# Four buffers for split weight parts, raw parts in the raw weights' place, and all attention constants ahead of batch 0

## The chip, the cores and the metric

One Trainium2 chip, one core of it. The metric is the device time of one execution in microseconds. The core's engines are TensorE (PE, with its weight loads as PEld), VectorE (DVE), ScalarE (ACT), GpSimd (POOL) and SyncE (SP), which here issues all transfers.

## What is computed

A macaron block over x of shape (8, 512, 256):

```python
x = x + 0.5 * ffn(layernorm(x), ...)
x = x + attention(layernorm(x), ...)
x = x + 0.5 * ffn(layernorm(x), ...)

# ffn: weights rounded to an 8-bit float, 256 -> 768 -> 256
gate = silu((x @ q(gate_w)) * gate_scale)
up = (x @ q(up_w)) * up_scale
return ((gate * up) @ q(down_w)) * down_scale

# attention: 16 heads of 128; q, k, v = silu(conv4(x @ W)); per token and head
sk = einsum('bhij,bhj->bhi', St, k_)
Sn = a_ * St - b_ * (sk - v_) k_^T
o_ = einsum('bhij,bhj->bhi', Sn, q_)
# then a norm over the head, a gate sigmoid(x @ Wg), and @ Wo
```

## The kernel before

The stream of eight batches of 512 tokens stays in SBUF. There are two phases, each a block with one instruction list for each engine; the order of every list is written out by hand, and semaphores join them. The second phase (`attention_phase`) runs the attention in steps of 128 tokens by four heads, with the last feed-forward layer in its tail. The change doesn't touch it.

`first_phase` runs the first feed-forward layer and, one or two batches behind, the second norm and the decay rows. Its unit is `turn(b)`, one for each engine and batch:

- DVE first converts the three feed-forward weights (`wraw` to `wq16`, 1536 columns each, six instructions each, at L474 to L481), with `low(0, 0)` and `stats(0, 1)` between the first and the second. Then it takes statistics, multiplies gate and up (`hidden`, L388), and scales the down product (L399).
- PE does `gate`, `up` (L642) and `down` (L660) for six tiles of 128 hidden columns a batch, and transposes (L614). `down(b, m)` needs POOL's lower half of the hidden tile, and there are three hidden buffers.
- ACT normalises (L508), takes silu (L528), and rounds the hidden tile to 16 bits (`hidden_high`, L537).
- POOL computes the roots for the norms (`root`, L298 to L303), the lower half of each hidden tile (`low`, L311), and adds the result to the stream (`added`, L321).

Beside this the attention's weights are split into two 16-bit halves. There are 20 parts of 128 x 1024 columns, three a turn. SP loads part x into `raw[:, x % 4]` (L182); ACT writes the upper half (`part_high`, L555) and DVE the lower one (`part_low`, L438). Parts 0 to 4 go straight into the attention's tiles; the others go to `pairs[:, x % 2]`, from which SP stores them in HBM (`save_part`, L190). ACT's part x waits for the store of part x - 2. In ACT's list `part_high(b + 1, 0)` stands between `high(0, b + 1)` and `normed(0, b + 2)`, and silu of the next batch comes behind them.

POOL also makes the constants of the attention phase: `attention_constants` (12 instructions: identities, a first mask, zeros of 3072 16-bit columns in `y16`) behind turn 0, and `level_constants(li)` (six levels, 10 instructions each) behind each of turns 1 to 6. Each of these instructions waits for the one before (`chain`). A level builds its mask in `blocks` (32 bits) and copies it to a 16-bit tile.

Of the kernel before, what the change touches and what calls it, by code (L numbers as in the profile page):

```python
# [61 lines left out]
def first_phase(nc, x_in, stream, z16, kit, scratch, w):  # L62

    with ExitStack() as ctx:
        def sb(name, shape, dt=F32):
            return ctx.enter_context(nc.sbuf_tensor("f_" + name, shape, dt))

        def sem(name):
            return ctx.enter_context(nc.semaphore("f_" + name))
# [30 lines left out]
        wabh = sb("wabh", [P, KT, 2 * NH], F16); wabl = sb("wabl", [P, KT, 2 * NH], F16)  # L100
        bab = sb("bab", [2 * NH, 1])
        ab = sb("ab", [2 * NH, 2, NC, CX]); gx = sb("gx", [NH, 2, NC, CX])
        heads0 = sb("heads0", [NH, NC, CX]); blocks = sb("blocks", [P, P])
        raw = sb("raw", [P, RAW, PART]); pairs = sb("pairs", [P, 2, 2, PART], F16)

        def of_norms(name):

# [3 lines left out]
        s_x = [sem(f"dma_tokens{i}") for i in range(3)]  # L111
        s_out = [sem("dma_out0"), sem("dma_out1")]
        s_save = sem("dma_saved"); s_wd = sem("weights_ready"); s_prm = sem("dma_conv")
        s_part = [sem(f"dma_part{i}") for i in range(RAW)]; s_pair = [sem("dma_pair0"), sem("dma_pair1")]
        a_part = sem("act_part"); d_part = sem("dve_part")
        s_const = sem("constants"); s_q = sem("quantise_step"); s_made = sem("pool_made")
        p_z = of_norms("pe_z")
# [17 lines left out]

        def part_pair(x):

            return pair_tiles(kit, x) if x < KINDS else pairs[:, x % 2]

        def part_of(b, k):  # L140

# [9 lines left out]
        @block.sync  # L151
        def _(sp):
            def load_x(b):
                sp.dma_start(stream[:, b], x_tok[b]).then_inc(s_x[min(b, 2)], 16)

            def load_columns(dst, name):
                sp.dma_start(dst[:, :], w[name].rearrange("(m p) -> p m", p=P),
                             allow_slow_non_contiguous=True).then_inc(s_small, 16)

            def store_rows(b):  # L160

                if b < 0:
                    return
                g = b % 2
                sp.wait_ge(d_ab, b + 1)
                for h in range(HG):
                    sp.dma_start(a_to[h, b], ab[U * h:U * (h + 1), g]).then_inc(s_out[g], 16)
                sp.wait_ge(d_g, b + 1)
                for h in range(HG):
                    sp.dma_start(g_to[h, b], gx[U * h:U * (h + 1), g]).then_inc(s_out[g], 16)  # L170

            def load_part(x):

                group, kind = divmod(x, KINDS)
                dst = raw[:, x % RAW]
                if kind < KINDS - 1:
                    src = w[("Wk", "Wq", "Wv", "Wg")[kind]].rearrange("(k p) (g n) -> g p k n", p=P, g=HG)[group]
                    dst = dst.rearrange("p (k n) -> p k n", k=KT)
                else:
                    src = w["Wo"].rearrange("(g u p) n -> g p u n", p=P, u=U)[group]  # L180
                    dst = dst.rearrange("p (u n) -> p u n", u=U)
                sp.dma_start(dst, src).then_inc(s_part[x % RAW], 16)  # L182

            def save_part(x):

                if x is None:
                    return
                sp.wait_ge(d_part, x + 1)
                if x >= KINDS:
                    sp.dma_start(w_pairs[x], pairs[:, x % 2]).then_inc(s_pair[x % 2], 16)  # L190
                if x + RAW < PARTS:
                    load_part(x + RAW)

            load_x(0)
            for i, (name, rows) in enumerate((("gate_w", KT), ("up_w", KT), ("down_w", MT))):
                sp.dma_start(wraw[:, i * KT * FF:(i + 1) * KT * FF].rearrange("p (k n) -> p k n", k=rows),
                             w[name].rearrange("(k p) n -> p k n", p=P)).then_inc(s_w[i], 16)
                if i == 0:
                    load_x(1)
            sp.dma_start(wab[:, :, 0:NH], w["Wa"].rearrange("(k p) n -> p k n", p=P)).then_inc(s_small, 16)  # L200
            sp.dma_start(wab[:, :, NH:], w["Wb"].rearrange("(k p) n -> p k n", p=P)).then_inc(s_small, 16)
            sp.dma_start(bab[0:NH, :], w["ba"].rearrange("(p o) -> p o", o=1)).then_inc(s_small, 16)
            sp.dma_start(bab[NH:, :], w["bb"].rearrange("(p o) -> p o", o=1)).then_inc(s_small, 16)
            load_columns(gs, "gate_scale")
            load_columns(us, "up_scale")
            sp.dma_start(hds[:, :], w["down_scale"].rearrange("(o n) -> o n", o=1).broadcast_to([P, H]))\
                .then_inc(s_small, 16)
            for b in range(2, B):
                load_x(b)
            for i, k in enumerate("kqv"):  # L210
                sp.dma_start(prm[:, i, :, 0:TAPS], w[k + "cw"].rearrange("(h p) t -> p h t", p=P))\
                    .then_inc(s_prm, 16)
                sp.dma_start(prm[:, i, :, TAPS], w[k + "cb"].rearrange("(h p) -> p h", p=P),
                             allow_slow_non_contiguous=True).then_inc(s_prm, 16)
            for x in range(RAW):
                load_part(x)
            sp.wait_ge(s_wd, 4)
            sp.dma_start(w_saved, wq16[:, :]).then_inc(s_save, 16)
            sp.dma_start(lnwn[:, :], w["ln_w"].rearrange("(p o) -> p o", o=1)).then_inc(s_prm, 16)
            sp.dma_start(lnb[:, :], w["ln_b"].rearrange("(p o) -> p o", o=1)).then_inc(s_prm, 16)  # L220
            for t in range(1, B + 2):
                save_part(part_of(t, 0))
                store_rows(t - 2)
                save_part(part_of(t, 1))
                save_part(part_of(t, 2))
            sp.wait_ge(s_save, 16)
            sp.wait_ge(s_prm, 16 * 8)
            for g in range(2):
                sp.wait_ge(s_pair[g], 16 * len([x for x in range(KINDS, PARTS) if x % 2 == g]))
                sp.wait_ge(s_out[g], rows_stored(B // 2))  # L230

        @block.gpsimd
        def _(pool):
# [14 lines left out]
            def chain(ins):  # L248

                made[0] += 1  # L250
                ins.then_inc(s_made, 1)
                pool.wait_ge(s_made, made[0])

            def fill(out, value, test, base, pattern, mult):
                chain(nc.gpsimd.affine_select(out=out, in_=out, compare_op=test, fill=value, base=base,
                                              pattern=pattern, channel_multiplier=mult))
# [17 lines left out]

            def level_constants(li):

                if not 0 <= li < NL:
                    return
                mb, y16 = LEVELS[li], kit["y16"]
                nb = P // (2 * mb)  # L280

                blk = blocks[:, :].rearrange("p (b two m) -> p b two m", two=2, m=mb)[:, :, 0, :]
                chain(nc.gpsimd.memset(blocks[:, :], 0.0))
                chain(nc.gpsimd.memset(blk, -1.0))
                fill(blk, 0.0, ALU.is_ge, -mb, [[-2 * mb, nb], [0, mb]], 1)
                fill(blk, 0.0, ALU.is_ge, 2 * mb - 1, [[2 * mb, nb], [0, mb]], -1)
                fill(blocks[:, :], -1.0, ALU.not_equal, 0, [[-1, P]], 1)
                chain(nc.gpsimd.tensor_copy(kit["masks"][:, li].rearrange("p (b m) -> p b m", m=mb), blk))
                for u in range(U):
                    chain(nc.gpsimd.tensor_copy(halves(y16[:, li, u], mb, 1), halves(kit["ident"][:, :], mb, 1)))  # L290

            def root(n, e):

# [39 lines left out]
                added(b)  # L333

            root(0, 0)
            root(0, 1)
            for b in range(0, B + 2):
                turn(b)
                if b == 0:
                    attention_constants()  # L340
                level_constants(b - 1)

        @block.vector
        def _(dve):
# [156 lines left out]
        def _(act):  # L501
# [46 lines left out]
            def part_high(b, k):  # L548
                x = part_of(b, k)
                if x is None:  # L550
                    return
                act.wait_ge(s_part[x % RAW], 16 * (x // RAW + 1))
                if x >= KINDS + 2:
                    act.wait_ge(s_pair[x % 2], 16 * len(range(KINDS + (x - KINDS) % 2, x, 2)))
                nc.scalar.activation(part_pair(x)[:, 0], raw[:, x % RAW], ACT.Copy, scale=WS).then_inc(a_part, 1)  # L555

            def turn(b):
# [1508 lines left out]
def pair_tiles(kit, x):  # L2066

    group, kind = divmod(x, KINDS)
    if kind < 3:
        return kit["kqv16"][:, :, kind].rearrange("p w k u d -> p w (k u d)")  # L2070
    if kind == 3:
        return kit["gate16"][:, :].rearrange("p w k u d -> p w (k u d)")
    return kit["wo16"][:, group % WO_SLOTS].rearrange("p w u n -> p w (u n)")
# [48 lines left out]
```

## Time and profile before

| | |
|---|---|
| median of 3 runs | 2467.68 us (2467.63 to 2468.91) |
| the profiled execution | 2468.06 us |
| its span | 2466.3 us |
| mean granted TensorE clock | 0.987 |
| busy of the span: PE, DVE, ACT, POOL | 96%, 82%, 74%, 74% |
| first phase | to about 238 us |

The span runs from the first to the last instruction of the core. A granted clock of 1.00 is 2.4 GHz and 0.50 is 1.2 GHz. Busy time of an engine says nothing by itself of what bounds a stage; idle time with what ended it, in the order of time, does.

### The profile page before, as it was taken

What the parts mean: (1) busy time and instruction counts of PE and PEld (TensorE: products, weight loads), DVE (VectorE), ACT (ScalarE), POOL (GpSimd) and SP (SyncE); (2) the same over time, 40 slices, a digit from 0 to 9 for tenths busy, and PEclk for the clock granted to TensorE, in tenths of its full rate; (3) what the DMA queues carried; (4) which work ended last, traced back from release to release, by engine and by line L of the source; (5) the groups of instructions that cost most, each with busy time, mean ns of one, the idle gap of its engine ahead of it and who ended that gap; (6) DMA issues with size and microseconds to landing.
All of it is one profiled execution on the core that took longest, in us unless ns stands there. A gap on an engine that the chain in (4) does not pass through costs nothing.

```text
span 2466.3 us, 64137 instructions
## 1 busy us (share of the span) xinstructions
PE 2357.2 (96%) x24496; PEld 1827.6 (74%) x24496; DVE 2017.2 (82%) x4246; ACT 1817.0 (74%) x3566; POOL 1818.9 (74%) x1973
## 2 busy tenths in 40 slices
PE   5897899999999999999999999999999999997898
PEld 2554578788888878888888888888788787886655
DVE  7775888888888888888888888888888888885453
ACT  3674677777777777777777777777777777775564
POOL 3774577777777777777877777777877777776565
PEclk9998999999999999999999999999999999998999
DMA  6241011111121111111211111111211121111001
GB/s 165 88 146 45 27 32 28 27 32 32 32 58 49 32 32 32 32 31 29 49 57 32 32 32 30 29 28 40 66 32 32 36 46 28 29 32 22 12 27 44
DMA packets 72833, 103.59 MB, mean 42 GB/s; under 512 B 21456, under 2 KB 33744, under 8 KB 72400
## 3 DMA queue, kind: packets, MB, share of 16 engines
q1 hardware_dynamic: 72528, 99.48, 15.9%
q8 instruction: 197, 3.23, 0.5%
q14 instruction: 108, 0.88, 0.1%
HBM read 85.69 MB, written 13.77 MB: 40 GB/s over the span
## 4 chain that ended last, share of the span: by engine, by line
PE 81%; DVE 6%; issue 1%; POOL 1%; ACT 1%; DVEq 0%; POOLq 0%; ACTq 0%
PE a_bank L1887 25%; PE a_bank L1867 7%; PE a_bank L1676 5%; PE a_bank L1690 5%; PE a_bank L1829 5%; PE a_bank L1828 4%; PE a_bank L1811 3%; PE a_bank L1722 3%; PE a_bank L1736 3%; PE a_bank L1734 3%; PE a_bank L1957 3%; DVE a_prod L1140 3%; PE a_bank L1759 2%; PE a_bank L1846 2%; PE a_bank L1749 2%; PE a_bank L1699 2%
## 5 line engine op out<-in xcount | busy, mean ns | idle before, releaser
L1887 PE MATMUL a_bank<-k_z,k_kqv 128*128 128x512 f16 x2304 | 597.9, 380 | 10.7 <-DVE a_kb L1233 4.2
L1462 ACT ACTIVATE a_inv<-a_bank 128x512 f16<-128x512 f32 x640 | 383.4, 599 | 216.9 <-PE a_bank L1736 201.5
L1164 DVE TENSOR_TENSOR k_y<-a_bank,k_masks 128x256 f16<-128x256 f32 x768 | 318.7, 415 | 134.9 <-PE a_bank L1722 131.1
L1887 PEld LDWEIGHTS a_bank<-k_z,k_kqv 128*128 128x128 f16 x2304 | 197.9, 98 | 139.8 <-DVE a_kb L1233 6.2
L912 POOL TENSOR_TENSOR k_diag<-k_ident,k_bcol 128x512 f32<-128x512 f32 x128 | 133.0, 1039 | 224.1 <-DVE a_prod L1140 209.1
L1233 DVE SCALAR_TENSOR_TENSOR a_kb<-a_bank,k_prm,a_kb 128x511 f32<-128x511 f32 (+2 forms) x384 | 282.7, 737 | 14.6 <-ACT a_kb L1406 14.3
L1233 DVE SCALAR_TENSOR_TENSOR a_vb<-a_bank,k_prm,a_vb 128x511 f32<-128x511 f32 (+2 forms) x384 | 283.7, 739 | 0.1
L1233 DVE SCALAR_TENSOR_TENSOR a_qb<-a_bank,k_prm,a_qb 128x511 f32<-128x511 f32 (+2 forms) x384 | 282.8, 737 | 0.5 <-ACT a_qb L1406 0.3
L1736 PE MATMUL a_bank<-a_inv,k_y 128*128 128x64 f16 x3072 | 271.8, 193 | 3.8 <-DVE k_y L1164 3.8
L1734 PE MATMUL a_bank<-k_y,a_inv 128*128 128x64 f16 x2560 | 236.5, 193 | 5.6 <-DVE k_y L1164 3.1
L1722 PEld LDWEIGHTS a_bank<-a_inv,a_am 128*128 128x128 f16 x3072 | 169.1, 98 | 92.6 <-ACT a_inv L1462 2.0
L1736 PEld LDWEIGHTS a_bank<-a_inv,k_y 128*128 128x128 f16 x3072 | 207.4, 98 | 37.6 <-DVE k_y L1164 4.6
L1734 PEld LDWEIGHTS a_bank<-k_y,a_inv 128*128 128x128 f16 x2560 | 197.4, 98 | 44.6 <-DVE k_y L1164 18.5
L924 POOL TENSOR_TENSOR a_am<-a_at,k_ident 128x512 f16<-128x512 f32 x128 | 163.6, 1278 | 80.6 <-DVE a_at L1149 80.6
L1000 POOL TENSOR_SCALAR a_gb<-a_gb 128x512 f32<-128x512 f32 x128 | 219.6, 1716 | 1.2 <-ACT a_gb L1426 1.2
L1722 PE MATMUL a_bank<-a_inv,a_am 128*128 128x64 f16 x3072 | 215.9, 193 | 1.4 <-ACT a_inv L1462 1.2
L1887 PE MATMUL a_bank<-k_z,k_gate 128*128 128x512 f16 x768 | 200.8, 379 | 0.2 <-DVE a_vb L1233 0.2
L1487 ACT ACTIVATE a_on<-a_bank,a_shift,a_rstd 128x128 f32<-128x128 f32 x512 | 192.2, 463 | 0.7 <-POOL a_shift L992 0.7
L1867 PE MATMUL a_bank<-k_wo,a_oh 128*128 128x256 f16 x1024 | 189.3, 273 | 2.1 <-POOL a_ol L1016 2.1
L1829 PE MATMUL a_bank<-a_wv,a_mix 128*128 128x128 f32 x1024 | 185.8, 279 | 0.7 <-DVE a_wv L1183 0.7
L1140 DVE TENSOR_TENSOR_SCAN a_prod<-a_decay,k_diag 128x516 f32<-128x516 f32 x128 | 181.9, 1421 | 2.1 <-ACT a_kdec L1437 2.1
L1009 POOL TENSOR_TENSOR a_oa<-a_oa,a_gb 128x512 f32<-128x512 f32 x128 | 163.1, 1274 | 21.0 <-ACT a_oa L1496 17.3
(178 smaller groups left out, 6638.7 us busy)
## 6 DMA issues: line engine op xcount, KB each, us to landing
a_decay<-decay_rows SPq DMA_DIRECT2D x128, 258.0 KB, 3.7
a_cum<-cumulative_rows SPq DMA_DIRECT2D x96, 258.0 KB, 3.6
weight_pairs<-f_pairs SPq DMA_DIRECT2D x15, 512.0 KB, 2.9
k_kqv<-weight_pairs SPq DMA_DIRECT2D x9, 512.0 KB, 4.8
stream<-in_L_attn_x SPq DMA_DIRECT2D x8, 512.0 KB, 7.1
out<-stream SPq DMA_DIRECT2D x8, 512.0 KB, 2.9
f_raw<-in_L_attn_Wk SPq DMA_DIRECT2D x4, 512.0 KB, 4.7
f_raw<-in_L_attn_Wq SPq DMA_DIRECT2D x4, 512.0 KB, 5.1
```

Of the source, the lines that this page charges most:

```text
L1000: nc.gpsimd.tensor_scalar(gb[:, n % 2, j], gb[:, n % 2, j], 1.0, None, ALU.add).then_inc(m["pool_one"], 1)
L1140: nc.vector.tensor_tensor_scan(prod[:, :], decay[:, :], diag[:, :, :].rearrange("p u x -> p (u x)"), 0.0, ALU.mult, ALU.add).then_inc(m["d ...
L1164: nc.vector.tensor_tensor(even(y16[:, j], mb), bank[LEV[par]][:, 0:U * C // 2].rearrange("p (u b m) -> p u b m", u=U, m=mb), masks[:, j].r ...
L1233: nc.vector.scalar_tensor_tensor(out=dst[:, d:S], in0=bank[PJ[j % 2]][:, 0:S - d], scalar=prm[:, i, U * (n // B) + j, TAPS - 1 - d:TAPS - ...
L1462: nc.scalar.activation(both, bank[LEV[par]][:, :].rearrange("p (two b m) -> p two b m", two=2, m=mb), ACT.Copy).then_inc(m[f"act_lev{par}" ...
L1487: ins = nc.scalar.activation(on[:, u], bank[OUT][:, u * D:(u + 1) * D], ACT.Identity, bias=shift[:, u:u + 1], scale=rstd[:, u:u + 1])
L1722: mm = pe.matmul(at_half(LEV[par], 0, u), am16[:, par, u], halves(t16[par][:, u], mb, 0), start=True, stop=True)
L1734: pe.matmul(at_half(LEV[par], 0, u), tt16[par][:, u], halves(y16[:, j, u], mb, 0), start=True, stop=True)
L1736: mm = pe.matmul(at_half(LEV[par], half, u), y16[:, j, u], halves(tt16[par][:, u], mb, 1), start=True, stop=True)
L1829: mm = pe.matmul(units(OUT)[:, u], mix[:, t % 2, u], wv[:, u], start=not c, stop=True)
L1867: mm = pe.matmul(bank[SUM][:, 0:H], o[:, u], wo16[:, group % WO_SLOTS, wh, u], start=(u == 0 and wh == 0 and o is oh), stop=(u == U - 1 an ...
L1887: mm = pe.matmul(bank[PJ[j % 2]][:, :], wt, z16[:, zh, k, cols], start=(x == 0), stop=(x == 5))
```

## The change

Three edits in the first phase. `pairs` has four buffers where it had two, with a semaphore each. `raw`, which was a tensor of its own, becomes the first 4096 columns of `wraw`, so that the loads of the first four raw parts now stand behind SP's wait for the converted feed-forward weights. POOL makes all constants ahead of its turns: the shared ones and level 0 between the roots of batch 0 and batch 1, the other five levels behind the root of batch 1. A level now builds its mask in the 16-bit tile itself (8 instructions where there were 10) and copies the 16-bit identity.

```diff
-        heads0 = sb("heads0", [NH, NC, CX]); blocks = sb("blocks", [P, P])
-        raw = sb("raw", [P, RAW, PART]); pairs = sb("pairs", [P, 2, 2, PART], F16)
+        heads0 = sb("heads0", [NH, NC, CX])
+        raw = wraw[:, 0:RAW * PART].rearrange("p (r n) -> p r n", r=RAW); pairs = sb("pairs", [P, RAW, 2, PART], F16)
...
-                    sp.dma_start(w_pairs[x], pairs[:, x % 2]).then_inc(s_pair[x % 2], 16)
+                    sp.dma_start(w_pairs[x], pairs[:, x % RAW]).then_inc(s_pair[x % RAW], 16)
...
+            sp.wait_ge(s_wd, 4)
             for x in range(RAW):
                 load_part(x)
-            sp.wait_ge(s_wd, 4)
             sp.dma_start(w_saved, wq16[:, :]).then_inc(s_save, 16)
...
             def level_constants(li):
...
-                chain(nc.gpsimd.memset(blocks[:, :], 0.0))
-                chain(nc.gpsimd.memset(blk, -1.0))
-                fill(blk, 0.0, ALU.is_ge, -mb, [[-2 * mb, nb], [0, mb]], 1)
-                fill(blk, 0.0, ALU.is_ge, 2 * mb - 1, [[2 * mb, nb], [0, mb]], -1)
-                fill(blocks[:, :], -1.0, ALU.not_equal, 0, [[-1, P]], 1)
-                chain(nc.gpsimd.tensor_copy(kit["masks"][:, li].rearrange("p (b m) -> p b m", m=mb), blk))
+                mask = kit["masks"][:, li].rearrange("p (b m) -> p b m", m=mb)
+                chain(nc.gpsimd.memset(mask, -1.0))
+                fill(mask, 0.0, ALU.is_ge, -mb, [[-2 * mb, nb], [0, mb]], 1)
+                fill(mask, 0.0, ALU.is_ge, 2 * mb - 1, [[2 * mb, nb], [0, mb]], -1)
+                fill(mask, -1.0, ALU.not_equal, 0, [[-2 * mb, nb], [-1, mb]], 1)
                 for u in range(U):
-                    chain(nc.gpsimd.tensor_copy(halves(y16[:, li, u], mb, 1), halves(kit["ident"][:, :], mb, 1)))
+                    chain(nc.gpsimd.tensor_copy(halves(kit["y16"][:, li, u], mb, 1),
+                                                halves(kit["ident16"][:, :], mb, 1)))
...
             root(0, 0)
+            attention_constants()
+            level_constants(0)
             root(0, 1)
+            for li in range(1, NL):
+                level_constants(li)
             for b in range(0, B + 2):
                 turn(b)
-                if b == 0:
-                    attention_constants()
-                level_constants(b - 1)
...
-                if x >= KINDS + 2:
-                    act.wait_ge(s_pair[x % 2], 16 * len(range(KINDS + (x - KINDS) % 2, x, 2)))
+                if x >= KINDS + RAW:
+                    act.wait_ge(s_pair[x % RAW], 16 * ((x - KINDS) // RAW))
```

## Rows read from the trace of the kernel before

**Rows 1.** Windows between starts of the adds: length, busy of each engine (instructions), clock, DMA.

```profile
54.40:77.02 22.62, 19.36 (x114) 11.56 (x113) 14.43 (x31) 16.25 (x29) 18.10 (x28) 0.92 0.13 44
77.02:100.63 23.61, 20.96 (x128) 12.10 (x126) 17.81 (x35) 17.15 (x29) 19.58 (x26) 1.00 0.23 73
100.63:123.96 23.33, 21.93 (x128) 12.73 (x126) 17.93 (x35) 14.04 (x23) 17.89 (x26) 0.93 0.37 121
123.96:148.02 24.06, 21.96 (x128) 12.73 (x127) 17.83 (x35) 16.91 (x28) 17.37 (x26) 0.93 0.43 132
148.02:171.96 23.94, 21.95 (x128) 12.75 (x127) 17.83 (x35) 16.96 (x28) 17.27 (x26) 0.93 0.43 139
171.96:194.11 22.15, 20.27 (x128) 12.26 (x127) 16.98 (x29) 16.85 (x28) 15.30 (x23) 1.00 0.43 139
194.11:215.96 21.85, 19.77 (x120) 11.26 (x119) 14.88 (x25) 12.84 (x21) 15.68 (x23) 1.00 0.20 75
```

**Rows 2.** Timeline of PE: start, us, instruction, idle before it and its releaser.

```profile
44.73 0.27 PE L660 MATMUL f_bank<-f_wq,f_hh 128*128 128x256 f16 x1
...
64.15 0.40 PE L660 MATMUL f_bank<-f_wq,f_hh 128*128 128x256 f16 x1 [2.69 <-POOL f_hl L311]
...
127.93 0.62 PE L642 MATMUL f_bank<-f_zh,f_wq 128*128 128x512 f16 x2 [2.10 <-ACT f_sg L528]
128.38 1.03 PE L642 MATMUL f_bank<-f_zl,f_wq 128*128 128x512 f16 x2
...
175.71 0.61 PE L642 MATMUL f_bank<-f_zh,f_wq 128*128 128x512 f16 x2 [1.88 <-ACT f_sg L528]
```

**Rows 3.** Timeline of ACT, two conversions of weight parts.

```profile
51.98 1.06 ACT L555 ACTIVATE k_kqv<-f_raw 128x1024 f16<-128x1024 f32 x1
...
124.28 1.06 ACT L555 ACTIVATE f_pairs<-f_raw 128x1024 f16<-128x1024 f32 x1 [2.62 <-DMA weight_pairs<-f_pairs]
```

**Rows 4.** The page's transfers: count, KB each, median us to landing.

```profile
weight_pairs<-f_pairs SPq DMA_DIRECT2D x15, 512.0 KB, 2.9
...
f_raw<-in_L_attn_Wk SPq DMA_DIRECT2D x4, 512.0 KB, 4.7
```

**Rows 5.** Timeline of DVE and POOL in the first 40 us.

```profile
16.28 1.29 DVE L379 TENSOR_TENSOR f_zl<-f_bank,f_zh 128x512 f16<-128x512 f32 x2 [0.90 <-ACT f_zh L520]
...
20.18 0.99 DVE L475 TENSOR_SCALAR f_wexp<-f_wexp 128x1536 f32<-128x1536 f32 x1
20.43 1.60 POOL L301 TENSOR_TENSOR f_rstd<-f_var,f_nhalf 128x4 f32<-128x4 f32 x1
21.20 1.76 DVE L476 TENSOR_TENSOR f_wraw<-f_wraw,f_wexp 128x1536 f32<-128x1536 f32 x1
22.11 0.91 POOL L303 TENSOR_TENSOR f_shift<-f_nmean,f_rstd 128x4 f32<-128x4 f32 x1
...
34.14 1.76 DVE L481 TENSOR_TENSOR f_wq<-f_wraw,f_wexp 128x1536 f16<-128x1536 f32 x1
...
38.53 1.15 POOL L311 TENSOR_TENSOR f_hl<-f_hid,f_hh 128x512 f16<-128x512 f32 x1 [15.51 <-ACT f_hh L537]
```

**Rows 6.** Timelines of POOL and DVE around the constants.

```profile
56.84 0.21 POOL L261 MEMSET k_ident<- 128x128 f32 x1
...
58.50 2.66 POOL L265 MEMSET k_y<- 128x3072 f16 x1
...
60.20 1.21 DVE L438 SCALAR_TENSOR_TENSOR k_kqv<-f_raw,k_kqv 128x1024 f16<-128x1024 f32 x1
...
62.94 1.15 POOL L311 TENSOR_TENSOR f_hl<-f_hid,f_hh 128x512 f16<-128x512 f32 x1
...
100.63 3.48 POOL L321 TENSOR_TENSOR stream<-stream,f_scaled 128x512 f32<-128x512 f32 x2 [1.91 <-DVE f_scaled L399]
101.07 1.92 DVE L438 SCALAR_TENSOR_TENSOR f_pairs<-f_raw,f_pairs 128x1024 f16<-128x1024 f32 x1
...
106.12 1.13 POOL L290 CAST k_y<-k_ident 128x64 f16<-128x64 f32 x4
```

More of the change, by code:

```diff
@@ L113, in first_phase @@
         s_save = sem("dma_saved"); s_wd = sem("weights_ready"); s_prm = sem("dma_conv")
-        s_part = [sem(f"dma_part{i}") for i in range(RAW)]; s_pair = [sem("dma_pair0"), sem("dma_pair1")]
+        s_part = [sem(f"dma_part{i}") for i in range(RAW)]; s_pair = [sem(f"dma_pair{i}") for i in range(RAW)]
         a_part = sem("act_part"); d_part = sem("dve_part")
@@ L136, in part_pair @@
         def part_pair(x):
-            return pair_tiles(kit, x) if x < KINDS else pairs[:, x % 2]
+            return pair_tiles(kit, x) if x < KINDS else pairs[:, x % RAW]
         def part_of(b, k):
@@ L227, in _ @@
             sp.wait_ge(s_prm, 16 * 8)
+            for x in range(RAW):
+                sp.wait_ge(s_pair[x], 16 * len([y for y in range(KINDS, PARTS) if y % RAW == x]))
             for g in range(2):
-                sp.wait_ge(s_pair[g], 16 * len([x for x in range(KINDS, PARTS) if x % 2 == g]))
                 sp.wait_ge(s_out[g], rows_stored(B // 2))
@@ L275, in level_constants @@
             def level_constants(li):
-                if not 0 <= li < NL:
-                    return
-                mb, y16 = LEVELS[li], kit["y16"]
+                mb = LEVELS[li]
                 nb = P // (2 * mb)
-                blk = blocks[:, :].rearrange("p (b two m) -> p b two m", two=2, m=mb)[:, :, 0, :]
-                chain(nc.gpsimd.memset(blocks[:, :], 0.0))
-                chain(nc.gpsimd.memset(blk, -1.0))
-                fill(blk, 0.0, ALU.is_ge, -mb, [[-2 * mb, nb], [0, mb]], 1)
-                fill(blk, 0.0, ALU.is_ge, 2 * mb - 1, [[2 * mb, nb], [0, mb]], -1)
-                fill(blocks[:, :], -1.0, ALU.not_equal, 0, [[-1, P]], 1)
-                chain(nc.gpsimd.tensor_copy(kit["masks"][:, li].rearrange("p (b m) -> p b m", m=mb), blk))
+                mask = kit["masks"][:, li].rearrange("p (b m) -> p b m", m=mb)
[3 more added lines that the diff above has]
+                fill(mask, -1.0, ALU.not_equal, 0, [[-2 * mb, nb], [-1, mb]], 1)
                 for u in range(U):
-                    chain(nc.gpsimd.tensor_copy(halves(y16[:, li, u], mb, 1), halves(kit["ident"][:, :], mb, 1)))
+                    chain(nc.gpsimd.tensor_copy(halves(kit["y16"][:, li, u], mb, 1),
+                                                halves(kit["ident16"][:, :], mb, 1)))
             def root(n, e):
```

## The prediction

> **What bounds the kernel now.** I read the page first, then busy time cut at the moments where POOL starts to add a batch's feed-forward result to the stream, then the timelines of PE, ACT, POOL and DVE with what each waited for, and last the transfers. The change touches only the first phase, the first 238 us or so. From 238 us on, where the long attention phase runs with its own order, no instruction differs, so I take that part as fixed and look for the difference in when the first phase ends.
>
> [Rows 1] give the turns of that phase, one batch each: 22.62, 23.61, 23.33, 24.06, 23.94, 22.15 and 21.85 us. I call them turns 1 to 7; turn 0 ends at 54.40. In the sixth PE stands idle once, 1.88 us at its end [rows 2], and its granted clock is 1.00 throughout; 22.15 - 1.88 = 20.3 us is what I take as the length of a turn whose PE is never late and whose clock never drops. PE is the bound to which the turns can shrink: DVE is busy 17 to 18 us and ACT 14 to 17 us of each [rows 1].
>
> What keeps turns 2 to 6 above 20.3 us? At the ends of turns 3, 4 and 5 PE waits 2.10, 1.99 and 1.88 us (first and last of the three in [rows 2]) for ACT's silu tile. ACT is late there because converting a weight part stood 2.62 us in front of it, waiting for a store of split weights [rows 3]: the two buffers take turns, so a part waits for the store of the part two before it, and such a store takes 2.9 us from issue to landing [rows 4]. After the wait of 2.10 us the granted clock falls from 2.4 to 1.2 GHz: a pair of 512-column products takes 1.03 us where it took 0.62 us [rows 2], and turns 3 to 5 show a mean clock of 0.93 [rows 1]. A mean of 0.93 over 24 us is 1.7 us of clock lost.
>
> In turn 1 PE waits 2.69 us, until 64.15, for POOL's first lower half [rows 2]. POOL was making the attention constants from 56.84 to 62.94 [rows 6]; the clock falls after that too (0.92 for the turn).
>
> **The change, part by part.**
>
> *Four split buffers.* ACT's wait for the store of x-2 becomes one for x-4, stored more than a turn earlier, so it goes. Each of turns 2 to 6 falls towards 20.3 us. Small waits stay whose cause is neither edit, so I take 21.0 us. The five sum to 117.1 us now and to 105.0 then: 12.1 us gained. Turn 7 has no normalisation of a next batch and converts two parts; I take 0.6 us there. Together -12.7 us. Bounds: at 20.3 us each it is -16.2 us; if each turn gives back only its PE waits of about 2 us in turns 3 to 5, with the clock loss unchanged, -6 us.
>
> *Raw parts in the feed-forward raw weights' place.* The first four loads are issued behind the last conversion (its last long instruction ends at 35.90 [rows 5]; the small weights follow within about 1 us) instead of at about 31 us. Four issues later, w_saved and two small loads follow on SP's queue; nobody reads those before the sixth turn. A raw load lands 4.7 us after issue [rows 4]; even with four of them sharing the engines, all are there by about 46 us, and ACT first reads one at 51.98 [rows 3]. Cost 0, hidden behind turn 0; without that cover it would be some 10 us. Copying the 16-bit identity in place of the 32-bit one I also put at 0: the same 64 columns.
>
> *Constants ahead of batch 0's rows.* This removes 6.1 us of POOL (56.84 to 62.94) from the start of turn 1 and about 3.1 us from each later turn: the adds end at 104.11 (100.63 + 3.48) and level 1's last copy at 107.25 [rows 6]. Its new place is from 10.9 us, behind the first root. Without block memset and mask copy a level costs about 2.4 us, level 0, whose runs are two elements long, about 2.8 (estimates from the 3.1). Unhindered: 10.9 + 6.0 + 2.8 + 1.6 (root of batch 1) + 5 x 2.4 = 33.3 us, before POOL is first wanted at 38.53 [rows 5]: cost 0. That is one bound.
>
> I don't take it, because DVE converts the feed-forward weights until 35.9 us almost without a gap, and there POOL is held. The power issued at 20.43 under DVE's 20.18 to 21.17 ends at 22.03, 1.60 us for some 1.0 elsewhere; the multiply issued at 22.11 ends at 23.02, just after DVE's 21.20 to 22.96 [rows 5]. So one POOL instruction that reads goes in at each DVE boundary. A memset does not need this: 58.50 to 61.16 lies over DVE's 60.20 to 61.41 and both keep their lengths [rows 6].
>
> The sum: boundaries at about 12.6 and 13.6 us let in the first select and the copy. From 15.38 DVE waits, then reads PSUM (16.28 [rows 5]) and takes statistics, until about 19.2, one conversion instruction ahead of 20.18. In this gap the long memset and the other small ones and two selects pass: the shared constants are done at about 19. The next 12 boundaries take level 0's three selects and four copies, the root of batch 1 and two instructions of level 1. DVE is held in turn by each (its 1.21 us instruction took 1.92 beside POOL's adds [rows 6]); for 64 columns I take 0.1 us each, 1.2 us in all, so DVE ends the conversions at 37.1. The root of batch 1 ends at about 34.3, then ACT needs about 2.1 us to normalise and 0.7 us for the first silu: 37.1 too, so it delays nothing more. From 37.1 POOL runs freely: 1.9 us of level 1 and 4 x 2.4 give 48.6. First lower half: 38.53 becomes 48.6.
>
> That rule has a page: in the Trainium skill, "SBUF — State Buffer", section "Who interferes with whom", the port pair that VectorE and GpSimd share is a lock, and whoever starts first keeps it for the whole instruction. The power in [rows 5] disagrees, since DVE's 21.20 instruction kept its 1.76 us beside it; with full-length holds of 0.25 to 0.45 us the conversions would end some 2 us later and the forecast would be about 2 us higher.
>
> What is late next: everything from PE's first down product, at 44.73 [rows 2], on. PE has done all that lies before it and idles from about 45 us; the half is there at 49.75 (1.15 us [rows 5]). From that product to the adds was 9.7 us (44.73 to 54.40); the idle clock costs 1.7 us as in the turns above: the adds of turn 0 start at 61.1, 6.7 us late. Turn 1: PE was ready for the first half 7.1 us after the adds (64.15 - 2.69 - 54.40), so it is ready at 68.2, and the half is there, since POOL is free. From 64.15 to 77.02 was 12.9 us at a dropped clock, 11.2 without that: 79.4 against 77.02, so +2.4 us. The constants' places in turn 1 give back 4.3 us of the 6.7.
>
> **Sum:** +2.4 - 12.7 = -10.3 us. Against the profiled execution's own 2468.06 (span 2466.3) that is 2457.8; the median of the runs is 0.4 us lower, and I forecast **2458 us**.
>
> **Rivals.** Within 0.2%, 4.9 us, is what a measurement of this kernel can't tell from no change.
>
> *POOL is not held at the start.* For: unhindered it is done at 33.3 us. Against: the two held instructions of [rows 5]. Then turn 0 ends at 54.4, PE is ready at 61.5, turn 1 ends at 72.7 (-4.3), and -4.3 - 12.7 = -17: 2451 us. It also stands for a milder hold.
>
> *Another wait takes the place of the stores.* DVE holds 17 to 18 us of a 21 us turn and shares its inputs with POOL; the parts' lower halves run beside POOL's adds at 1.92 us. If turns 2 to 7 give 6 us only, the time is 2468.06 + 2.4 - 6 = 2464.5, about the edge of no change; with a start 2 us worse, 2466.5.
>
> *The constants cost more than they give (slower).* One mechanism: after 37.1 us some 30 selects and copies stand in front of the first lower half with no cover, and on 16-bit strided tiles their price is not in the trace (only 32-bit selects and 32-to-16 copies are). The gain of 10.3 us is gone when each costs 0.3 us more, twice today's; at 0.5 us more the time is about 2473. Against: copies that write 16 bits already cost what 32-bit selects do.
>
> *Nothing changes:* the stores' wait is removed but start and turns cancel. It is the middle of the second rival, and counted there.
>
> **How the numbers follow.** Forecast 0.48 (own range 2454 to 2463), no hold 0.16, another wait 0.28 (half of it over 2462.8), slower 0.08. Faster by over 0.2% (under 2462.8): 0.47 + 0.16 + some of the second rival, 0.69 together; within it 0.24; slower 0.07. The range from 2450 to 2467 leaves out the slow rival and the ends.
>
> **What would show it.** Right: no ACT wait on stores after the first four splits; turns 2 to 6 of 20.5 to 21.3 us with a clock near 1.00; selects and copies one to each conversion until 37 us; the first lower half near 48.6 us; the first phase ending 10 us earlier. Wrong: a first lower half before 40 us or after 54 us, conversions ending after 39 us, turns still above 22 us, or a different attention phase.

## The result and the profile after

The changed kernel takes 2457.88 us (median, 2455.13 to 2459.36) against 2467.65 us of the kernel before in the same measurement: a ratio of 0.9958, 95% interval 0.9945 to 0.9971. The forecast was 2458, so the total is right. Part of that is luck: the first phase gained 13.3 us where 10.3 were forecast, and 3.0 of them are not in the total. And the reason that was given for most of the gain was only one of two.

Busy time of the changed kernel, cut at the starts of POOL's adds (turns 1 to 7), then the rest of the first phase, then the second phase in three pieces (columns as in [rows 1]):

```profile
59.92:79.33 19.41, 17.82 (x114) 11.07 (x113) 14.35 (x31) 16.25 (x29) 14.15 (x17) 1.00 0.17 52
79.33:99.93 20.60, 20.18 (x128) 12.23 (x126) 17.54 (x35) 16.51 (x28) 14.44 (x17) 1.00 0.27 82
99.93:120.54 20.61, 20.27 (x128) 12.30 (x127) 17.54 (x35) 16.73 (x30) 14.45 (x17) 1.00 0.43 139
...
161.75:182.36 20.61, 20.27 (x128) 12.33 (x127) 16.41 (x29) 15.51 (x26) 13.53 (x13) 1.00 0.48 150
182.36:202.63 20.27, 19.57 (x120) 11.34 (x119) 15.18 (x25) 11.90 (x20) 12.04 (x13) 1.00 0.21 82
...
224.59:2141.18 1916.59, 1902.10 (x21098) 1522.86 (x21099) 1676.31 (x3561) 1493.88 (x2988) 1477.61 (x1544) 1.00 0.15 36
2141.18:2272.99 131.81, 116.68 (x1229) 95.55 (x1228) 95.31 (x218) 90.15 (x184) 90.65 (x101) 0.91 0.13 26
2272.99:2456.00 183.01, 162.76 (x1166) 107.39 (x1164) 82.46 (x176) 98.44 (x173) 106.97 (x116) 0.97 0.08 28
```

Against [rows 1]: turns 2 to 6 take 20.60 or 20.61 us each, for 22.2 to 24.1; PE is busy 20.27 of 20.61 us in turns 3 and 6, at a clock of 1.00; POOL's busy time in turns 2 to 5 was 17.3 to 19.6 us and is about 14.4. The same three pieces of the second phase in the kernel before, cut at the same instructions (the scan of the decays that is 121st and the last of the 128):

```profile
237.93:2154.28 1916.35, 1901.02 (x21098) 1522.79 (x21099) 1676.37 (x3562) 1495.41 (x2988) 1477.25 (x1544) 1.00 0.15 36
2154.28:2284.84 130.56, 114.39 (x1232) 94.00 (x1231) 95.32 (x218) 90.25 (x185) 90.67 (x101) 0.93 0.12 26
2284.84:2466.30 181.46, 160.80 (x1163) 106.15 (x1161) 82.35 (x176) 98.14 (x173) 106.98 (x116) 0.98 0.09 28
```

The second phase starts 13.34 us earlier (224.59 for 237.93), keeps all but 0.24 us of that over 1916 us, and gives back 1.25 and 1.55 us in its last two pieces, where the granted clock is 0.91 and 0.97 for 0.93 and 0.98. PE stands idle several times there, up to 5.07 us in one wait.

The front of the changed kernel, POOL's timeline:

```profile
18.77 2.66 POOL L256 TENSOR_SCALAR_AFFINE_SELECT k_masks<-k_masks 128x64 f16<-128x64 f16 x3
21.50 6.11 POOL L286 COPY k_y<-k_ident 128x64 f16<-128x64 f16 x4
27.70 0.87 POOL L295 TENSOR_TENSOR f_var<-f_mv,f_epsd 128x4 f32<-128x4 f32 x1
...
31.54 4.63 POOL L256 TENSOR_SCALAR_AFFINE_SELECT k_masks<-k_masks 128x64 f16<-128x64 f16 x3
36.23 1.21 POOL L286 COPY k_y<-k_ident 128x64 f16<-128x64 f16 x4
...
47.34 3.38 POOL L308 TENSOR_TENSOR f_hl<-f_hid,f_hh 128x512 f16<-128x512 f32 x3
```

and DVE's and PE's:

```profile
18.96 1.07 DVE L472 TENSOR_SCALAR f_wexp<-f_wraw 128x1536 int32<-128x1536 int32 x1
...
25.76 1.76 DVE L479 TENSOR_TENSOR f_wq<-f_wraw,f_wexp 128x1536 f16<-128x1536 f32 x1
...
34.19 1.76 DVE L479 TENSOR_TENSOR f_wq<-f_wraw,f_wexp 128x1536 f16<-128x1536 f32 x1
```

```profile
48.55 0.28 PE L658 MATMUL f_bank<-f_wq,f_hh 128*128 128x256 f16 x1 [4.10 <-POOL f_hl L308]
49.05 0.42 PE L658 MATMUL f_bank<-f_wq,f_hh 128*128 128x256 f16 x1
...
103.00 0.60 PE L640 MATMUL f_bank<-f_zh,f_wq 128*128 128x512 f16 x2 [0.34 <-DVE f_hid L386]
```

Four copies take 6.11 us where DVE converts and 1.21 us behind the last of them: POOL is held, as forecast, one reading instruction to a conversion. The first lower half comes at 47.34 us. DVE is hardly held in return: its two-input conversions keep 1.76 us, and the last ends at 35.95, 0.05 us later than before. (This stretch began 0.25 us earlier, so the conversions lost about 0.3 us.)

PE waits 4.10 us for that half and restarts at full clock, 0.28 us a product. Then the clock falls: until 52.4 us a product takes 0.42 us, and the mean granted clock from 48.55 to 52.41 is 0.56. From 48.55 to the adds at 59.92 it is 0.85, against 1.00 for the same work before. This work takes 11.37 us where it took 9.67. In turns 3 to 6 the only wait of PE is one of 0.34 us.

### The profile page after: what moved, and what is told of

Read it like the earlier page. It is cut to its first block, busy times and chain, and to the rows that moved or that the text cites. A ratio compares the mean times of both kernels' runs of the same rounds, so it can differ in the third digit from the quotient of the medians.

```text
span 2456.0 us, 64125 instructions
## 1 busy us (share of the span) xinstructions
PE 2354.8 (96%) x24496; PEld 1828.3 (74%) x24496; DVE 2015.9 (82%) x4246; ACT 1814.9 (74%) x3566; POOL 1824.1 (74%) x1961
## 4 chain that ended last, share of the span: by engine, by line
PE 81%; DVE 6%; issue 1%; POOL 1%; ACT 1%; DVEq 0%; POOLq 0%; ACTq 0%
PE a_bank L1885 25%; PE a_bank L1865 7%; PE a_bank L1674 5%; PE a_bank L1688 5%; PE a_bank L1827 5%; PE a_bank L1826 4%; PE a_bank L1809 3%; PE a_bank L1734 3%; PE a_bank L1720 3%; PE a_bank L1732 3%; PE a_bank L1955 3%; DVE a_prod L1138 3%; PE a_bank L1757 2%; PE a_bank L1844 2%; PE a_bank L1747 2%; PE a_bank L1697 2%
## 5 line engine op out<-in xcount | busy, mean ns | idle before, releaser
L1007 POOL TENSOR_TENSOR a_oa<-a_oa,a_gb 128x512 f32<-128x512 f32 x128 | 163.2, 1275 | 21.3 <-ACT a_oa L1494 17.3
```

## Experiments

All figures of this table but the last column are from the timelines of one profiled execution each; the time is a median of timed runs, and one run alone for the kernel with writes only. "Turns 2 to 6" is their sum. "First half" is the start of POOL's first lower half.

| kernel | first half | adds of turn 0 | turn 1 | turns 2 to 6 | first phase ends | time, us |
|---|---|---|---|---|---|---|
| before | 38.5 | 54.4 | 22.6 | 117.1 | 237.9 | 2467.44 to 2469.05 |
| changed | 47.3 | 59.9 | 19.4 | 103.0 | 224.6 | 2457.88; again: 2455.71 |
| raw parts' place alone | 38.2 | 54.3 | 22.6 | 115.4 | 236.2 | 2469.42 |
| buffers and place | 38.2 | 53.6 | 22.7 | 115.2 | 235.2 | 2466.94 |
| constants alone | 47.4 | 59.7 | 19.4 | 110.6 | 232.2 | 2464.22 |
| changed, levels 2 to 5 at the end | 38.7 | 53.7 | 19.4 | 103.0 | 218.5 | 2450.58 |
| changed, levels 1 to 5 twice | 60.0 | 73.2 | 19.4 | 103.0 | 238.2 | 2469.55 |
| changed, writes only | 38.4 | 53.9 | 19.4 | 103.0 | 218.6 | 2450.16 |
| levels 2 to 5 ahead of adds | 38.6 | 54.4 | 20.0 | 107.4 | 224.1 | 2456.51 |
| levels 2 to 5 behind adds | 38.6 | 53.7 | 19.4 | 110.9 | 226.2 | 2459.77 |

**Buffers without the constants.** The edits to `pairs`, `s_pair` and `raw`, on the kernel before; POOL's part as it was.

```diff
             root(0, 0)
-            attention_constants()
-            level_constants(0)
             root(0, 1)
-            for li in range(1, NL):
-                level_constants(li)
             for b in range(0, B + 2):
                 turn(b)
+                if b == 0:
+                    attention_constants()
+                level_constants(b - 1)
```

(against the changed kernel; `level_constants` is that of before)

> Four split buffers and the raw parts' new place, with the constants left where they were (behind turns 0 to 6). Theory 1 (the stores' wait is what lengthens turns 2 to 6): no ACT wait for a store, turn 1 stays 22.6 us with PE's wait of 2.7 us for the first lower half, turns 2 to 6 at about 20.9 us, first phase some 11 us shorter than before: about 2456.5 us. Rival (POOL's level constants at each turn's start would take the wait's place): turns 2 to 6 at about 22 us, about 2462 us.

Ratio to before 0.9993 (0.9984 to 1.0003): no difference that this measures, and neither theory. No ACT wait for a store is left, and yet turns 2 to 5 take 23.1 to 23.6 us. Windows of turns 3 and 4:

```profile
99.91:123.23 23.32, 20.78 (x128) 12.12 (x126) 17.81 (x35) 16.88 (x28) 19.28 (x26) 1.00 0.43 134
123.23:146.55 23.32, 20.79 (x128) 12.13 (x126) 17.82 (x35) 16.88 (x28) 19.29 (x27) 1.00 0.45 143
```

and rows of the turn from 146.55, all engines:

```profile
143.57 0.28 PE L661 MATMUL f_bank<-f_wq,f_hh 128*128 128x256 f16 x1 [0.93 <-POOL f_hl L312]
145.78 1.29 DVE L400 TENSOR_TENSOR f_scaled<-f_bank,f_hds 128x512 f32<-128x512 f32 x2 [1.56 <-PE f_bank L661]
146.55 3.48 POOL L322 TENSOR_TENSOR stream<-stream,f_scaled 128x512 f32<-128x512 f32 x2 [1.91 <-DVE f_scaled L400]
...
151.85 2.02 POOL L291 CAST k_y<-k_ident 128x64 f16<-128x64 f32 x4
153.95 1.15 POOL L312 TENSOR_TENSOR f_hl<-f_hid,f_hh 128x512 f16<-128x512 f32 x1
155.24 0.75 DVE L389 SCALAR_TENSOR_TENSOR f_hid<-f_bank,f_us,f_sg 128x512 f32<-128x512 f32 x1 [1.47 <-POOL f_hl L312]
156.82 2.07 ACT L509 ACTIVATE f_ztok<-stream,f_shift,f_rstd 128x256 f32<-128x256 f32 x4 [2.33 <-POOL f_shift L304]
...
163.63 1.84 POOL L304 TENSOR_TENSOR f_shift<-f_nmean,f_rstd 128x4 f32<-128x4 f32 x1
164.20 1.20 DVE L439 SCALAR_TENSOR_TENSOR f_pairs<-f_wraw,f_pairs 128x1024 f16<-128x1024 f32 x1
```

The waits that name POOL are now everywhere: PE 0.93 us, DVE 1.47 us, ACT 2.33 us. POOL is busy 19.3 us of the turn. Its longest wait, 1.91 us, is for the scaled product, which follows from its last lower half, and 1.06 us are for ACT's upper half of a hidden tile. So the chain runs through POOL around the turn: last half, down product, scaling, adds, constants, first half, root, next halves. What stands in it lengthens each turn.

Part of that chain is POOL being held by DVE. The multiply that ends a root takes 1.84 us here and ends 0.07 us after DVE's lower half of a weight part; the four copies took 2.02 us beside another such part. In the turns of the changed kernel this multiply takes 0.20 to 0.24 us, and four copies with nothing beside them take 1.13 us. No run takes this hold away alone, so its share of the 23.3 us is not shown.

**Constants without the buffers.** POOL's edit alone, on the kernel before.

```diff
-        raw = wraw[:, 0:RAW * PART].rearrange("p (r n) -> p r n", r=RAW); pairs = sb("pairs", [P, RAW, 2, PART], F16)
+        raw = sb("raw", [P, RAW, PART]); pairs = sb("pairs", [P, 2, 2, PART], F16)
```

(against the changed kernel, with the waits and SP's order of before)

> The constants ahead of batch 0 alone, with two split buffers and separate raw tiles. Theory 1: turn 0 ends 5.5 us later (59.9 for 54.4), turn 1 takes about 19.4 us for 22.6, turns 3 to 5 stay near 23.9 us because of the stores' wait: net +1 us, about 2468.5 us. Rival (the constants lengthened the turns, not the stores): turns 2 to 6 at 21 to 22 us and about 2461 us.

0.9984 (0.9975 to 0.9994), 4.8 us faster than before by the medians. Turns 0 and 1 are as theory 1 said (59.7, 19.4), the later ones are not. (The profiled execution, 2467.27 us, is the longest of its ten.) Turns 2 and 3 fall to 20.61 and 21.33 us: ACT's first wait for a store, 1.75 us, comes in turn 3. Turns 4 to 6 take 22.45, 22.40 and 23.84 us (the last at a clock of 0.93), with this wait in ACT and after it in PE:

```profile
143.62 1.06 ACT L552 ACTIVATE f_pairs<-f_raw 128x1024 f16<-128x1024 f32 x1 [2.65 <-DMA weight_pairs<-f_pairs]
...
147.28 0.60 PE L639 MATMUL f_bank<-f_zh,f_wq 128*128 128x512 f16 x2 [1.98 <-ACT f_sg L525]
```

Together, these two kernels settle where the gain came from. By the sum of turns 2 to 6, and against the 115.4 us of the kernel with the place alone, the buffers give 0.2 us, the constants 4.8, and both 12.4. (Against the one profile of the kernel before, 117.1 us, it is 1.9, 6.5 and 14.1.) Either of two causes is enough to keep a turn above 22 us.

**The raw parts' place alone.**

```diff
-        raw = sb("raw", [P, RAW, PART]); pairs = sb("pairs", [P, 2, 2, PART], F16)
+        raw = wraw[:, 0:RAW * PART].rearrange("p (r n) -> p r n", r=RAW); pairs = sb("pairs", [P, 2, 2, PART], F16)
...
+            sp.wait_ge(s_wd, 4)
             for x in range(RAW):
                 load_part(x)
-            sp.wait_ge(s_wd, 4)
```

> Raw parts in the feed-forward raw weights' place and nothing else. Theory 1: the first conversion of a part still finds its data, no time: 2467.7 us. Rival (later loads are late, or collide with the store of the converted weights): ACT waits for a raw part in turn 0 or 1, and 2470 us or more.

1.0002 (0.9992 to 1.0011): no time. No ACT wait for a raw part shows in turns 0 to 7. This kernel also shows how far one profiled execution of the kernel before can mislead: its turns 4 and 5 take 23.27 and 23.23 us with the clock at 1.00, where [rows 1] have 24.06 and 23.94 at 0.93. The longest ACT waits for a store are alike, 2.50 and 2.51 us for 2.51 and 2.40. So with the clock full these turns are 0.8 and 0.7 us shorter, not the 1.7 that the prediction reads from the clock, and what is left, 23.2 to 23.3 us, is about what the buffers alone leave too.

**The changed kernel again,** without an edit.

> The changed kernel again, for its last 220 us. Theory 1 (the granted clock falls at other moments in the last feed-forward stretch, and this is where 3 of the 13.3 us gained by 225 us went): the first phase ends within 0.3 us of the same time, the steps up to 2230 us keep their distance to it, and the runs differ by up to 4 us, the longer ones with the lower mean clock. Rival (the change costs 3 us in the second phase each time): the last stretch is as long in each run, and the total within 1 us of 2457.9.

2455.71 us (2454.78 to 2456.52), 0.9946 (0.9931 to 0.9961) of a kernel before that took 2469.05 there: 13.3 us, all that the first phase gained. The phase ends at 224.52, 0.07 us from the first time. Its second phase took 2230.2 us for 2231.4, and 1.05 us of the difference lie behind the last scan (181.96 us for 183.01). The runs of this measurement differ by 1.7 us, those of the first one by 4.2, and there the longest has a mean clock of 0.987 and the shortest 0.990. Over all profiled kernels, whose second phases hold the same instructions, that phase took 2228.4 to 2233.3 us. The kernel before that stands in [rows 1] is the shortest of them; the kernel with the place alone took 2230.0, like this one. So the 3 us are not a cost that the change has each time.

**Levels 2 to 5 at the end.**

```diff
-            for li in range(1, NL):
-                level_constants(li)
+            level_constants(1)
             for b in range(0, B + 2):
                 turn(b)
+            for li in range(2, NL):
+                level_constants(li)
```

> The changed kernel with levels 2 to 5 made behind the last turn, where POOL was idle for 15 us, instead of ahead of batch 0. Theory 1 (POOL's constants stand in front of the first lower half): the first lower half at 38.2 us for 47.3, turn 0 ends at 54.4 for 59.8, the turns stay at 20.6 us, the levels (9.7 us) fit in POOL's idle time, and the first phase ends 5.4 us earlier. Rival (the end has no room, or turn 1 takes the time back because its own waits grow): 0 to 2 us gained.

2450.58 us (2450.03 to 2453.14), 0.9928 of before (0.9914 to 0.9943): the fastest complete kernel of the study, 17 us under before. The first phase ends 6.1 us earlier. POOL's timeline:

```profile
36.26 1.21 POOL L286 COPY k_y<-k_ident 128x64 f16<-128x64 f16 x4
38.68 1.16 POOL L308 TENSOR_TENSOR f_hl<-f_hid,f_hh 128x512 f16<-128x512 f32 x1 [1.21 <-ACT f_hh L536]
...
203.40 0.15 POOL L281 MEMSET k_masks<- 128x64 f16 x1
...
212.09 1.14 POOL L286 COPY k_y<-k_ident 128x64 f16<-128x64 f16 x4
218.46 1.04 POOL L911 TENSOR_TENSOR k_diag<-k_ident,k_bcol 128x512 f32<-128x512 f32 x1 [5.23 <-POOLq L64]
```

Level 1 is done 1.21 us before the first half could start; the other four take 9.8 us at the end, and 5.23 us of idle time are left.

**Levels 1 to 5 twice.**

```diff
-            for li in range(1, NL):
+            for li in list(range(1, NL)) * 2:
```

> The changed kernel with levels 1 to 5 made twice ahead of batch 0, to double a suspected cost. Theory 1: the first lower half comes 12.1 us later, at 59.4 us, and the first phase ends 12 us later, one to one. Rival (PE has slack in turns 0 and 1 that takes part of it): 8 us or less.

The first half comes 12.7 us later and the phase ends 13.6 us later, 2469.55 us for 2457.88: one to one and a little more, and as slow as the kernel before (1.0006, 0.9997 to 1.0015). PE's first down product waits long and starts at the low clock already (0.40 us for 0.28):

```profile
61.23 0.40 PE L658 MATMUL f_bank<-f_wq,f_hh 128*128 128x256 f16 x1 [16.82 <-POOL f_hl L308]
```

**Writes only.** The selects and copies of the six levels are memsets on the same tiles; the masks and identities of the attention are left out.

```diff
                 chain(nc.gpsimd.memset(mask, -1.0))
-                fill(mask, 0.0, ALU.is_ge, -mb, [[-2 * mb, nb], [0, mb]], 1)
-                fill(mask, 0.0, ALU.is_ge, 2 * mb - 1, [[2 * mb, nb], [0, mb]], -1)
-                fill(mask, -1.0, ALU.not_equal, 0, [[-2 * mb, nb], [-1, mb]], 1)
+                for _ in range(3):
+                    chain(nc.gpsimd.memset(mask, -1.0))
                 for u in range(U):
-                    chain(nc.gpsimd.tensor_copy(halves(kit["y16"][:, li, u], mb, 1),
-                                                halves(kit["ident16"][:, :], mb, 1)))
+                    chain(nc.gpsimd.memset(halves(kit["y16"][:, li, u], mb, 1), 0.0))
```

> The changed kernel with all selects and copies of the six levels replaced by memsets on the same tiles (so the masks and identities of the attention are left out; its output is not the reference's). Theory 1 (POOL is held by DVE's conversions only where it reads SBUF, or where DVE runs a one-input conversion at double rate): level 0's four copies, 6.11 us before, take under 2 us, the root of batch 1 starts near 22 us for 27.7, and the first lower half is at 38.2 us. Rival (each POOL instruction is held, reading or not): one memset a conversion, the root near 27 us as before.

```profile
18.73 2.21 POOL L283 MEMSET k_masks<- 128x64 f16 x3
20.99 0.78 POOL L285 MEMSET k_y<- 128x64 f16 x4
21.86 0.84 POOL L293 TENSOR_TENSOR f_var<-f_mv,f_epsd 128x4 f32<-128x4 f32 x1
...
31.27 0.78 POOL L285 MEMSET k_y<- 128x64 f16 x4
...
38.37 1.16 POOL L306 TENSOR_TENSOR f_hl<-f_hid,f_hh 128x512 f16<-128x512 f32 x1 [0.46 <-ACT f_hh L533]
```

Theory 1 holds, both halves of it. Under DVE's conversions with two inputs in SBUF four memsets take 0.78 us where four copies took 6.11. Three memsets of 0.15 us take 2.21 us at 18.73, where DVE runs two one-input conversions of 1536 columns in 0.93 and 0.96 us: those hold writes too. The last conversion ends at 35.61 here; POOL's reading instructions cost DVE the 0.34 us up to 35.95.

The Trainium skill's "SBUF — State Buffer", section "Who interferes with whom", has it so: GpSimd's writes are free beside a VectorE instruction of two SBUF inputs and blocked beside one in a two-port mode. The traces agree, if the one-input conversions, 0.96 us for columns that take 1.76 with two inputs, are in such a mode.

**Levels 2 to 5 in front of the adds,** and then **behind them** (both with level 1 ahead of batch 0).

```diff
                 low(b, 5)
+                if 1 <= b <= NL - 2:
+                    level_constants(b + 1)
                 added(b)
```

```diff
             for b in range(0, B + 2):
                 turn(b)
+                if 1 <= b <= NL - 2:
+                    level_constants(b + 1)
```

> Shared constants and levels 0 and 1 ahead of batch 0, levels 2 to 5 in turns 1 to 4 in front of POOL's adds, where POOL waits 2.2 us for DVE. Theory 1 (what the constants cost in a turn is their place between the adds and the first lower half): turns 1 to 4 lengthen by 0.2 to 0.5 us each at most, and the first phase ends 4 to 5 us earlier than in the changed kernel. Rival (POOL's total work in a turn counts): turns 1 to 4 at 22 us or more.

> As the kernel with levels 2 to 5 in front of the adds of turns 1 to 4, but behind these adds, at the start of turns 2 to 5, where the kernel before had them. Theory 1 (POOL's chain through a turn sets its length as soon as 2.4 us more stand in it, four split buffers or not): turns 2 to 5 at 22.3 to 23.0 us, the others at 20.6, the first phase ending at about 226 us. Rival (place doesn't matter, the sum of POOL's work does): 21.8 us as in front of the adds, ending at 223.

In front of the adds, turns 1 to 4 carry a level: turn 1 takes 20.0 us, the others 21.7 to 21.8. Turn 5, with none, still takes 21.4. Behind the adds, turns 2 to 5 carry one and take 22.5 to 22.7 us. That is 1.2 and 2.0 us more than without. Two windows of each, in front and then behind:

```profile
74.45:96.19 21.74, 20.50 (x127) 12.17 (x126) 17.18 (x35) 16.83 (x29) 18.94 (x25) 1.00 0.24 76
96.19:118.00 21.81, 20.56 (x127) 12.25 (x126) 17.24 (x35) 16.71 (x29) 19.00 (x24) 1.00 0.47 146
```

```profile
73.09:95.77 22.68, 20.78 (x128) 12.18 (x126) 17.80 (x35) 17.15 (x29) 18.79 (x24) 1.00 0.25 76
95.77:118.34 22.57, 20.79 (x128) 12.18 (x126) 18.80 (x35) 16.88 (x28) 18.66 (x24) 1.00 0.47 138
```

For the behind case theory 1 is right (22.3 to 23.0 forecast, phase end 226.2 for 226). For the one in front both theories missed (0.2 to 0.5 us more a turn, and 22 us or more; the phase ends at 224.1, 0.5 us before the changed kernel's and not 4 to 5): POOL's idle time of 2.24 us before the adds doesn't take in a level of 2.4 us for nothing. The place matters, by 0.8 us. POOL is busy 18.7 to 19.0 us in both, 4.2 to 4.6 more than in the changed kernel, though a level is 2.4: in turns 2 to 5 of both the multiply of a turn's second root takes 1.84 us for 0.20, also in turn 5 of the first kernel, where no level is left. So a POOL that is late also meets DVE's weight parts; that this is what lengthens turn 5 is likely, not shown.

Behind the adds, a level of 8 instructions (22.6 us a turn) stands against one of 10 in the buffers without the constants (23.3). Making a level shorter gives 0.7 us of the 2.7, taking it out of the turn the other 2.0.

## Why the prediction came out as it did

**Right, and shown.** The POOL side of the start: one reading instruction to a conversion, memsets passing beside the two-input conversions, the first half at 47.3 us (48.6), turn 0's adds at 59.9 (61.1), turn 1's at 79.3 (79.4). Doubling the levels moved the end one to one, and taking them out from in front of the first half gave 6.1 us back and 2450.6 us, near the 2451 that the prediction gives for a turn 0 that ends at 54.4. The clock after PE's first wait also fell as forecast: the work up to the adds took 1.70 us more, for 1.7. The new place of the raw parts costs nothing. The turns do shrink to what PE needs: 20.6 us, between the 20.3 and 21.0 that were weighed.

**Mis-sized, same mechanism.** DVE's conversions: about 0.3 us longer in all, not 1.2; the last ends at 35.95 for 37.1. All behind them comes as much earlier: the first half by 1.3 us, the adds of turn 0 by 1.2. Turns 2 to 6 gave 14.1 us for 12.1 (12.4 against the kernel with the place alone), and turn 7 1.6 for 0.6: it too had level 5 at its start and waits for stores in ACT.

**Wrong: the step "four split buffers ... each of turns 2 to 6 falls towards 20.3 us".** It gave all 12.1 us to the buffers and, of the constants, counted only turn 1 as relieved. The runs showed two bounds of nearly the same height: the stores' wait (22.4 us and more a turn when it is alone) and POOL's chain with the level constants in it (23.3 us). The buffers alone remove the first and gain nothing that can be measured; only with the second gone as well does PE set the turn. The rival "another wait takes the place of the stores" is what happened with the buffers alone. It named DVE's and POOL's holds, which are part of that chain, but not the constants, and it priced the pair of edits, not one. The sum was saved because the change made both edits.

A row of the kernel before already showed the second bound. Turn 2 takes 23.61 us at full clock, and no ACT wait for a store stands in it or before it (the first, 1.74 us, ends at 106.05). PE waits for POOL there, and POOL's multiply takes 1.85 us as in the buffers without the constants:

```profile
94.65 1.85 POOL L303 TENSOR_TENSOR f_shift<-f_nmean,f_rstd 128x4 f32<-128x4 f32 x1
...
97.66 0.28 PE L660 MATMUL f_bank<-f_wq,f_hh 128*128 128x256 f16 x1 [0.93 <-POOL f_hl L311]
```

The prediction counted this turn among those that the stores' wait lengthens. It also placed PE's three waits at the ends of turns 3 to 5; by the windows of [rows 1] they lie some 4 us into turns 4 to 6, and turn 3 has its clock of 0.93 with PE waits of 0.43 and 0.97 us only.

What misled was the reading of the sixth turn in [rows 1]: 22.15 less PE's one long wait of 1.88 us. Subtracting PE's last wait says how far PE's work would let the turn shrink; it doesn't say that whatever stands in POOL's list would have been done by then. POOL's busy time in turns 2 to 5, 17.3 to 19.6 us in [rows 1], was not set beside DVE's and ACT's.

**Wrong: the second phase is not a constant.** It came out 3.0 us longer than in the one profile of before, and over all profiles it varies by 4.9 us with no instruction changed. In the two profiles compared above, 2.8 of the 3.0 us lie in its last 315 us, where the mean clock is lower too. Why executions differ there was not traced further; it stays open why the first measurement gave 9.8 us and the second 13.3. The forecast of 2458 is thus 10.3 us of forecast gain meeting 13.3 of gain less 3 of the second phase. (The prediction's own sum, 2457.8 less 0.4 for the median, is 2457.4; it wrote 2458.)

## What to carry to other kernels

When two engines' lists close a loop around one turn, find what each would set as the turn's length before giving the gain to the wait that ends last: a wait that is visible in front of the bounding engine can hide a second chain of the same length, and then half a change measures as nothing. A turn that is long without the wait, here turn 2, is the sign to look for. Work that is done once belongs where its engine has nothing to do for anyone, here behind the last turn, and not merely earlier. And a part of the program that the change leaves alone still has a spread of its own; take it from several runs, not from one profile.

## What was not expected of the hardware

POOL's selects and copies slipped in between DVE's conversions almost free of charge to DVE: 1.76 us stayed 1.76 us for each two-input conversion of the changed kernel, and the largest lengthening was 0.11 us (0.96 to 1.07), though a select of 64 columns lasts about 0.25 us where nothing holds it. The other way round the price is high: a POOL multiply of 4 columns took 1.84 us for 0.20 and ended with a DVE instruction of 1.20 us. And the same instructions of the second phase took 2228.4 to 2233.3 us in the profiles here.
